# Four of the eight key tiles of each second query half leave TensorE's transposes: VectorE turns 32x32 squares, DRAM puts the squares in place

## The chip, the cores and the metric

The kernel runs on one core of a Trainium2 chip. The metric is the device time of one execution in microseconds (us), of which three were taken. One more execution was recorded by the hardware profiler; all rows below are from that one. Engines: PE is TensorE's matmul, PEld its weight load, DVE is VectorE, ACT is ScalarE, POOL is GpSimd, and SP is SyncE, which issues DMAs.

## The reference

Two layers are added to their input. x is (2, 1024, 512) in float32.

```python
xn = _layernorm(x)
# attention: 32 query heads of 128, 8 key/value heads, 4-bit weights with a scale for each group of 128 rows
q, k, v = [(qw - 8) * repeat(scales, 128)] products of xn, then rope on q and k
scores = q @ k.T / sqrt(128);  scores = where(causal, scores, finfo.min)
ctx = softmax(scores) @ v                       # float32
attn = ctx @ ((qw_o - 8) * repeat(scales_o, 128))
# linear layer: xn @ W_base.T + b_base, plus a top-2 mixture of 8 LoRA experts of rank 16
out = x + attn + ffn(xn)
```

The softmax over 1024 tokens is computed for 64 pairs of batch and query head (2 times 32), each with a causal mask.

## The kernel before

Every float32 product is made of three matmuls over a high and a low part (high times high, high times low, low times high). ACT makes the high part by a copy, DVE or POOL the low part by a subtraction.

Work is cut into 16 units (batch and key/value head), each with REP = 4 query heads. A head has two halves of 512 query tokens, c = 0 and c = 1. With causal masking, half 0 needs key tiles 0 to 3 and half 1 key tiles 0 to 7; tiles 0 to 3 of half 1 are full, tiles 4 to 7 hold the diagonal and get narrower (512, 384, 256 and 128 columns). For a head the steps on TensorE are:

- F: `project`, queries or keys of half c (12 matmuls of 512 columns), into one of the RING = 4 PSUM banks of `ring`. DVE makes three products for the rotary embedding (`terms`), POOL adds them (`rope_add`), ACT makes the high part (`rope_high`), POOL the low (`rope_low`).
- S: `scores` of query tile i against (i + 1) key tiles, 3 products. From i = 4 it takes two banks of `ring`. DVE copies it to `probs` with its mask and row maximum (`row_max`), ACT takes the exponential (`exps`).
- T: `turn`, up to four 128x128 transposes of probabilities for key tile j, into one of TURNS = 3 banks `turned`. ACT copies to `PT_high` (`high`), DVE subtracts for `PT_low` (`low`).
- V: `values`, the product of key tile j's probabilities and V, summed in the one bank `O_ps`. The first V of a half waits until DVE has taken the half before out of `O_ps` (`norm`, which multiplies by the reciprocal row sums in `R_sb`).
- O: `output`, context times output weights, added to Y by DVE (`add`). P: `rows_v`, rows of V for two units.

The order on TensorE is written by hand as strings of these letters: FIRST, EARLY and THIRD for half 0 of heads 0, 1 and 2, and 3; LATE and LAST for half 1. FIRST_P and LAST_P take the place of FIRST in even units and of LAST in odd ones. Every other engine runs one in-order queue. Its place for each operation comes from `behind(STEPS, us, kind)`, a rough clock of TensorE's steps: the operation is queued when the step is so many us old. A wait at the head of a queue holds all that stands behind it.

SP's queue holds all DMAs of the steady part: `load_weight` (two loads of 256 KB for each of 160 weights), `store_sums` and `load_sums` (the reciprocal sums go through DRAM to be spread over the partitions into `R_sb`). POOL scales each weight and splits it (four instructions, 3.8 us in sum).

## Time and profile before

| | us |
|---|---|
| device time, median of 3 | 2106.51 (2105.98 to 2108.94) |
| device time of the profiled execution | 2108.06 |
| its span, first to last instruction | 2106.3 |
| PE busy | 2084.7 (99%) |
| DVE / POOL / ACT busy | 1510.7 / 1213.4 / 993.5 |
| granted TensorE clock, mean | 0.998 |

The profiled execution's own time is 1.8 us over its span and 1.55 us over the median. Matmuls overlap in the trace (each has a duration that holds its way through the array), so what one costs is the distance from its start to the next start.

### The profile page before, as it was taken

The numbers are of one execution on the slowest core, as the hardware profiler recorded it, in microseconds if no ns is written. First come the engines' busy times: TensorE is split into PE (matmuls) and PEld (weight loads), VectorE is DVE, ScalarE is ACT, GpSimd is POOL, SyncE is SP. The second block draws the span as 40 slices with busy tenths as digits, with TensorE's granted clock in tenths as the row PEclk, the third lists the DMA queues.
The fourth block names the chain that finished last, engine by engine and source line by source line (L and its number), as shares of the span: only waits on it lengthen the run. The fifth ranks groups of instructions, "written<-read, shape, count | busy, mean of one in ns | idle before, by whom it ended". The sixth has DMA issues, their size and how long they took to land.

```text
span 2106.3 us, 31748 instructions
## 1 busy us (share of the span) xinstructions
PE 2084.7 (99%) x11690; PEld 1806.4 (86%) x11692; DVE 1510.7 (72%) x3056; ACT 993.5 (47%) x2199; POOL 1213.4 (58%) x1117
## 2 busy tenths in 40 slices
PE   8999999999999999999999999999999999999999
PEld 6888888888888888888888888888888888888887
DVE  6757776777767777677767777677776777767776
ACT  3145454554544545454444445454544545445453
POOL 3745665556655566456664666555665656646542
PEclk9999999999999999999999999999999999999999
DMA  6522222322312233232363422222231224313112
GB/s 222 156 41 61 58 69 56 61 56 56 81 46 57 59 61 76 44 67 58 61 149 80 114 59 63 49 71 61 56 78 34 71 46 79 73 31 70 36 41 66
DMA packets 160923, 145.88 MB, mean 69 GB/s; under 512 B 26368, under 2 KB 117248, under 8 KB 160256
## 3 DMA queue, kind: packets, MB, share of 16 engines
q1 hardware_dynamic: 157312, 137.80, 28.3%
q0 software_dynamic: 2112, 4.19, 0.6%
q8 instruction: 93, 1.52, 0.3%
q10 hardware_dynamic: 1344, 1.85, 0.3%
q14 instruction: 62, 0.51, 0.1%
HBM read 133.06 MB, written 10.75 MB: 68 GB/s over the span
## 4 chain that ended last, share of the span: by engine, by line
PE 94%; DVE 3%; POOL 1%; issue 1%; ACT 1%; DMA 0%; SPq 0%; DVEq 0%; POOLq 0%
PE ring L1123 43%; PE ring L1253 20%; PE O_ps L1123 19%; PE turned L1264 11%; POOL rope L683 1%; DVE rope L991 0%; POOL Q_low L691 0%; DVE rope L993 0%; DVE PT_low L924 0%; DVE stats L880 0%; DMA Y<-in_x 0%; DVE rope L992 0%; PE turned L1168 0%; ACT Q_high L736 0%; DVE xnT_low L924 0%
## 5 line engine op out<-in xcount | busy, mean ns | idle before, releaser
L736 ACT ACTIVATE PT_high<-turned 128x512 fp32r<-128x512 f32 (+3 forms) x771 | 359.2, 488 | 516.1 <-PE turned L1264 496.1
L790 ACT ACTIVATE probs<-probs,negmax 128x128 f32<-128x128 f32 (+7 forms) x512 | 398.1, 777 | 229.6 <-DVE negmax L1002 222.5
L924 DVE TENSOR_TENSOR PT_low<-turned,PT_high 128x512 fp32r<-128x512 f32 (+3 forms) x771 | 410.5, 555 | 117.0 <-ACT PT_high L736 108.6
L1002 DVE CUSTOM_DVE_ANT_0 probs<-ring,mask_row 128x128 f32<-128x128 f32 (+7 forms) x512 | 386.0, 754 | 83.1 <-PE ring L1253 74.2
L698 POOL TENSOR_TENSOR ctx_low<-ctx_f,ctx_high 128x512 fp32r<-128x512 f32 x128 | 165.4, 1292 | 410.0 <-ACT ctx_high L736 410.0
L1264 PE MATMUL turned<-ident,probs 128*128 128x128 f32 x2304 | 344.5, 273 | 0.0
L683 POOL TENSOR_TENSOR rope<-rope 128x512 f32<-128x512 f32 x160 | 206.9, 1293 | 177.0 <-DVE rope L993 175.9
L1264 PEld LDWEIGHTS turned<-ident,probs 128*128 128x128 f32 x2304 | 273.2, 140 | 35.5
L1123 PE MATMUL O_ps<-PT_high,V_high 128*128 128x512 f32 (+3 forms) x768 | 284.9, 371 | 7.1 <-DVE PT_low L924 7.1
L1043 DVE TENSOR_TENSOR Y<-ring,Y 128x512 f32<-128x512 f32 x256 | 177.0, 692 | 126.0 <-PE ring L1123 121.8
L1123 PE MATMUL O_ps<-PT_high,V_low 128*128 128x512 f32 (+3 forms) x768 | 265.9, 346 | 0.0
L1123 PE MATMUL O_ps<-PT_low,V_high 128*128 128x512 f32 (+3 forms) x768 | 265.1, 345 | 0.0
L1123 PE MATMUL ring<-xnT_high,W_high 128*128 128x512 f32 x640 | 255.2, 399 | 0.0
L1123 PE MATMUL ring<-xnT_high,W_low 128*128 128x512 f32 x640 | 250.0, 391 | 0.0
L1123 PE MATMUL ring<-xnT_low,W_high 128*128 128x512 f32 x640 | 249.5, 390 | 0.0
L1253 PE MATMUL ring<-K_high,Q_high 128*128 128x384 f32 (+5 forms) x768 | 236.7, 362 | 3.7 <-POOL Q_low L691 3.7
L1253 PE MATMUL ring<-K_low,Q_high 128*128 128x384 f32 (+5 forms) x768 | 221.4, 342 | 0.0
L1253 PE MATMUL ring<-K_high,Q_low 128*128 128x384 f32 (+5 forms) x768 | 221.3, 342 | 0.0
L691 POOL TENSOR_TENSOR Q_low<-rope,Q_high 128x512 fp32r<-128x512 f32 x128 | 165.5, 1293 | 94.3 <-ACT Q_high L736 93.1
L991 DVE TENSOR_TENSOR rope<-ring,cos_sb 128x512 f32<-128x512 f32 x160 | 110.7, 692 | 147.4 <-PE ring L1123 145.4
L649 POOL TENSOR_TENSOR W_low<-scl,W_high 128x512 fp32r<-128x512 f32 x160 | 206.8, 1292 | 13.3
L634 POOL TENSOR_TENSOR scl<-raw,scl 128x512 f32<-128x512 f32 x160 | 206.7, 1292 | 13.3
(115 smaller groups left out, 3861.1 us busy)
## 6 DMA issues: line engine op xcount, KB each, us to landing
R_sb<-row_sums SPq DMA_DIRECT2D x128, 256.0 KB, 4.1
raw<-in_qw_q SPq DMA_DIRECT2D x64, 256.0 KB, 4.8
scl<-in_scales_q SPq DMA_DIRECT2D x64, 256.0 KB, 8.6
raw<-in_qw_o SPq DMA_DIRECT2D x64, 256.0 KB, 4.5
scl<-in_scales_o SPq DMA_DIRECT2D x64, 256.0 KB, 4.8
raw<-in_qw_k SPq DMA_DIRECT2D x16, 256.0 KB, 4.5
scl<-in_scales_k SPq DMA_DIRECT2D x16, 256.0 KB, 6.1
raw<-in_qw_v SPq DMA_DIRECT2D x16, 256.0 KB, 4.4
```

The source lines that it names most:

```text
L634: own(nc.gpsimd.tensor_tensor(out=scl[:, n % 2, :], in0=as_float, in1=scl[:, n % 2, :], op=ALU.mult))
L649: nc.gpsimd.tensor_tensor(out=W_low[:, slot, :], in0=scl[:, n % 2, :], in1=W_high[:, slot, :].bitcast(f32), op=ALU.subtract).then_inc(w_do ...
L683: nc.gpsimd.tensor_tensor(out=rope_a[:, n % 2, :], in0=rope_a[:, n % 2, :], in1=rope_b[:, n % 2, :], op=ALU.add).then_inc(rope_sum, 1)
L691: nc.gpsimd.tensor_tensor(out=low[:, half(c)], in0=rope_a[:, n % 2, :], in1=high[:, half(c)].bitcast(f32), op=ALU.subtract).then_inc(rope_ ...
L736: return nc.scalar.activation(dst, src, ACT.Copy)
L790: nc.scalar.activation(probs[:, at], probs[:, at], ACT.Exp, bias=negmax[:, i:i + 1], scale=-1.0, accum_out=sums[:, i:i + 1]).then_inc(exp_ ...
L924: nc.vector.tensor_tensor(out=dst, in0=src, in1=high.bitcast(f32), op=ALU.subtract).then_inc(pt_low, 1)
L1002: nc.vector.tensor_tensor_reduce(probs[:, prob_at[i]:prob_at[i] + n], score_place(u, h, i), mask_row[:, TOKENS - n:TOKENS], -1.0, -MASKED, ...
L1043: nc.vector.tensor_tensor(out=Y[:, t, :], in0=place(step), in1=Y[:, t, :], op=ALU.add).then_inc(ring_read, 1)
L1123: mm = nc.tensor.matmul(dst, lhs, rhs, start=start and n == 0, stop=stop and n == len(terms) - 1)
L1253: mm = nc.tensor.matmul(ps[:, lo:hi], lhs[:, tile], keys[:, lo:hi], start=first, stop=last)
L1264: mm = nc.tensor.transpose(turned_place(step)[:, q * P:(q + 1) * P], probs[:, at:at + P], ident[:, :])
```

## The change

For half 1 of every head, key tiles 0 to 3 no longer pass through `turn`. Instead:

1. `scores` of tiles i = 4 to 7 read the first 512 keys in another order (four groups of 32 keys from each of four tiles: `p (j b k) -> p b j k`). Its two matmuls for each product are now 512 columns and the rest; they were two halves of the width.
2. After the exponential, DVE transposes the first 512 columns of the row in place, in squares of 32 (`turn_squares`, four for a head).
3. SP writes these 256 KB to DRAM (`move_out`, four for a head) and reads them back in four DMAs of 256 KB (`move_in`) with partition and block exchanged, in runs of 128 floats. All four stores have to land first.
4. ACT makes `moved_high` (two buffers) and POOL, no longer DVE, `moved_low`; four each for a head.
5. `values` of half 1 run in the order 0, 1, 4, 5, 6, 7, 2, 3. LATE and LAST hold four T in place of eight, and all eight S of the next head stand in them; before, four of the eight stood in the next EARLY.
6. To make room: `PT_low` has 2 buffers (3 before), so `low` waits for the V of two turns ago; W has 9 slots (11); `raw` and `rope_b` have one buffer (two), so a weight's load waits until POOL has scaled the one before.
7. `store_sums` and `row_sums_inverted` follow the first T that is left in a half.

```diff
-EARLY = "S T T F V S T V S S T O O V V"
-THIRD = "T S F T V S T S S T V V O O V"
-LATE = "S T T T S F V T V T V O V T T V T S S O V T V V V"
+FIRST = "F T T V T O T V F O V O V O"
+EARLY = "F T F T T O V O V O T O V V"
+THIRD = "F T F O T O V F T V T V O V F O"
+LATE = "S S T T V V S T V S T S V S V S V S V V"
+LAST = "T V S T T V S V S T V V S V S S S S V V"
+VALUES = ([0, 1, 2, 3], [0, 1, 4, 5, 6, 7, 2, 3])
+MOVED = 4
...
-            return (i + 1) * P // (2 if i >= 4 else 1)
+            return min(i + 1, MOVED) * P
...
+            def move_out(u, h, i):
+                n = head_of(u, h)
+                if seen.new(squared, 4 * n + i - 3):
+                    sp.wait_ge(squared, 4 * n + i - 3)
...
+                sp.dma_start(squares[n % 2][i - 4].rearrange("p (b n) -> p b n", b=4),
+                             row_squares(i).rearrange("p (b n) -> p b n", b=4)).then_inc(moved_out[i - 4], 16)
...
+            def move_in(u, h):
+                n = head_of(u, h)
+                for i in range(4):
+                    if seen.new(moved_out[i], 16 * (n + 1)):
+                        sp.wait_ge(moved_out[i], 16 * (n + 1))
...
+                back = squares[n % 2].rearrange("r (a k) (b n) -> b k (r a) n", a=4, b=4)
+                for b in range(4):
+                    sp.dma_start(moved[32 * b:32 * (b + 1), :, :, :].rearrange("p t j q -> p t (j q)"),
+                                 back[b]).then_inc(moved_in[n % 2], 16)
...
+            squares_out, squares_in = behind(STEPS, 4.5, "scores"), behind(STEPS, 6.5, "scores")
...
+                nc.gpsimd.tensor_tensor(out=low, in0=moved[:, :, j, :], in1=high.bitcast(f32),
+                                        op=ALU.subtract).then_inc(moved_done, 1)
...
+            def turn_squares(u, h, i):
+                need = score_number[u, h, i]
+                if seen.new(exp_done, need):
+                    dve.wait_ge(exp_done, need)
+                nc.vector.transpose(row_squares(i), row_squares(i)).then_inc(squared, 1)
...
-                at = slice(max(0, j - 4 * c) * P, HALF)
-                mm = product(O_ps[:, at], [(both(V_high, V_low, slice(None), u % 2, j),
-                                            both(PT_high, PT_low, slice(None), j % TURNS, at))],
-                             start=j == 0, stop=last)
...
+                if j < 4 * c:
+                    turned_tile = moved_high[:, j % 2, :], moved_low[:, j % 2, :]
```

**First place, DVE where an even unit ends and an odd one begins.** Before: the last row maximum of LAST (512 columns, tile 3), the context of the half (`ctx_f`), an `add`, a projection's three products, then the low part of FIRST's first turn.

```order
L1002 ISA probs,negmax<-ring,mask_row 128x512 [waits ring_full]
L1002 ISA negmax 128x1
L1032 TENSOR_TENSOR ctx_f<-O_ps,R_sb 128x512 [waits ctx_done,r_loaded,o_full]
L1043 TENSOR_TENSOR Y<-ring,Y 128x512 [waits ring_full]
L991 TENSOR_TENSOR rope<-ring,cos_sb 128x512 [waits rope_done,ring_full]
L992 TENSOR_TENSOR rope<-ring,sin_sb 64x512
L993 TENSOR_TENSOR rope<-ring,sin_sb 64x512
L924 TENSOR_TENSOR PT_low<-turned,PT_high 128x512 [waits pt_high]
```

Now, at the same place:

```order
L1156 STREAM_TRANSPOSE probs<-probs 128x512 [waits exp_done]
L1149 ISA probs,negmax<-ring,mask_row 128x1024 [waits moved_out3,ring_full]
L1149 ISA negmax 128x1
L1156 STREAM_TRANSPOSE probs<-probs 128x512 [waits exp_done] x3
L1184 TENSOR_TENSOR ctx_f<-O_ps,R_sb 128x512 [waits ctx_done,r_loaded,o_full]
L1129 TENSOR_TENSOR rope<-ring,cos_sb 128x512 [waits rope_done,ring_full]
L1133 TENSOR_TENSOR rope<-ring,sin_sb 64x512 [waits rope_sum]
L1134 TENSOR_TENSOR rope<-ring,sin_sb 64x512
L1062 TENSOR_TENSOR PT_low<-turned,PT_high 128x512 [waits valued,pt_high]
```

The widest row maximum and the square transposes, the last of which waits for the widest exponential, now stand ahead of that low part. On TensorE FIRST begins `F T T V` (it was `T F V`).

**Second place, SP in one head.** Now: four stores, the reciprocal sums of the next half 0, then the four loads, the next weight and the loaded sums.

```order
L569 DMA squares<-probs 128x512 [waits moved_in0,squared]
L569 DMA squares<-probs 128x512 [waits squared] x3
L544 DMA row_sums<-rinv 128x4 [waits r_loaded,rinv_ready]
L583 DMA moved<-squares 32x16x128 [waits moved_out3,moved_out2,moved_done,moved_out1,moved_out0]
L583 DMA moved<-squares 32x16x128 x3
L531 DMA raw<-in_qw_q 128x4x128 [waits scaled]
L535 DMA scl<-in_scales_q 128x4x128 [waits w_done]
L559 DMA R_sb<-row_sums 128x512 [waits ctx_made,r_stored]
```

Before, only the rows for sums and weights stood there. In most heads the sums' store stands ahead of the loads as here; in some it stands behind.

**Third place, TensorE where EARLY ends and LATE begins.** Now: S of tiles 0 and 1, two turns (seven transposes), then the first two V of the moved tiles.

```order
L1412 MATMUL ring<-K_high,Q_high 128x256 [waits ring_read]
L1412 MATMUL ring<-K_low,Q_high 128x256
L1412 MATMUL ring<-K_high,Q_low 128x256
L1423 MATMUL turned<-ident,probs 128x128 [waits exp_done]
L1423 MATMUL turned<-ident,probs 128x128 x6
L1278 MATMUL O_ps<-moved_high,V_high 128x512 [waits ctx_made,moved_done]
L1278 MATMUL O_ps<-moved_low,V_high 128x512
L1278 MATMUL O_ps<-moved_high,V_low 128x512
L1278 MATMUL O_ps<-moved_high,V_high 128x512 [waits moved_done]
```

Before, LATE had a projection (F, 12 matmuls) ahead of its first V. That V waits for two things: `ctx_made` (DVE has emptied `O_ps`) and `moved_done` (POOL's low part).

## Rows read from the trace of the kernel before

**Rows 1.** The page: busy time, and the chain that ended last by engine.

```profile
PE 2084.7 (99%) x11690; PEld 1806.4 (86%) x11692; DVE 1510.7 (72%) x3056; ACT 993.5 (47%) x2199; POOL 1213.4 (58%) x1117
...
PE 94%; DVE 3%; POOL 1%; issue 1%; ACT 1%; DMA 0%; SPq 0%; DVEq 0%; POOLq 0%
```

**Rows 2.** Busy time by stretch (us, busy and count by engine), two units' length.

```profile
489.00:738.00 249.00, 247.88 (x1394) 215.64 (x1393) 180.26 (x356) 120.86 (x268) 148.11 (x137) 1.00 0.26 60
```

**Rows 3.** Timeline of PE around two turns: start, us, engine, line, operation.

```profile
1035.58 0.39 PE L1123 MATMUL O_ps<-PT_high,V_low 128*128 128x512 f32 x1
1035.81 0.60 PE L1264 MATMUL turned<-ident,probs 128*128 128x128 f32 x4
1036.16 0.48 PE L1123 MATMUL O_ps<-PT_high,V_high 128*128 128x512 f32 x1
1036.48 0.40 PE L1123 MATMUL O_ps<-PT_low,V_high 128*128 128x512 f32 x1
```

**Rows 4.** Timeline of PE at scores of tiles 0 and 4.

```profile
1030.36 0.27 PE L1253 MATMUL ring<-K_high,Q_high 128*128 128x128 f32 x1
1030.47 0.27 PE L1253 MATMUL ring<-K_low,Q_high 128*128 128x128 f32 x1
...
1045.27 0.51 PE L1253 MATMUL ring<-K_high,Q_high 128*128 128x320 f32 x2
...
1045.91 0.46 PE L1253 MATMUL ring<-K_high,Q_low 128*128 128x320 f32 x2
```

**Rows 5.** Groups by line and shape, DVE: count, busy us, mean ns.

```profile
L924 DVE TENSOR_TENSOR PT_low<-turned,PT_high 128x512 fp32r<-128x512 f32 x387 | 260.9, 688 | 57.8 <-ACT PT_high L736 50.9
...
L1032 DVE TENSOR_TENSOR ctx_f<-O_ps,R_sb 128x512 f32<-128x512 f32 x128 | 138.6, 1083 | 25.0 <-PE O_ps L1123 23.8 <-issue 1.2
L992 DVE TENSOR_TENSOR rope<-ring,sin_sb 64x512 f32<-64x512 f32 x160 | 110.8, 693 | 2.1
...
L1002 DVE CUSTOM_DVE_ANT_0 probs<-ring,mask_row 128x1024 f32<-128x1024 f32 x64 | 78.4, 1225 | 18.1 <-PE ring L1253 17.4
...
L915 DVE MEMSET mask_row<- 128x448 uint32 x1 | 0.4, 432 | 0.0
```

**Rows 6.** The same view, ACT and POOL.

```profile
L736 ACT ACTIVATE Q_high<-rope 128x512 fp32r<-128x512 f32 x128 | 80.3, 627 | 117.9 <-POOL rope L683 116.9
L790 ACT ACTIVATE probs<-probs,negmax 128x1024 f32<-128x1024 f32 x64 | 73.6, 1150 | 23.7 <-DVE negmax L1002 23.7
...
L698 POOL TENSOR_TENSOR ctx_low<-ctx_f,ctx_high 128x512 fp32r<-128x512 f32 x128 | 165.4, 1292 | 410.0 <-ACT ctx_high L736 410.0
```

**Rows 7.** DMA view: SP's queue (packets, MB, share); issues (KB, us to landing).

```profile
q1 hardware_dynamic: 157312, 137.80, 28.3%
...
raw<-in_qw_q SPq DMA_DIRECT2D x64, 256.0 KB, 4.8
scl<-in_scales_q SPq DMA_DIRECT2D x64, 256.0 KB, 8.6
Y<-y_parked SPq DMA_DIRECT2D x2, 1024.0 KB, 5.0
out<-Y SPq DMA_DIRECT2D x8, 256.0 KB, 2.0
```

**Rows 8.** Timeline of SP: what issuing a DMA takes.

```profile
1035.36 0.43 SPq L495 DMA_DIRECT2D raw<-in_qw_v  x1
```

**Rows 9.** Timeline, a V that waits for a low part behind DVE's rope products.

```profile
478.66 0.60 PE L1264 MATMUL turned<-ident,probs 128*128 128x128 f32 x4
479.17 1.45 DVE L924 TENSOR_TENSOR PT_low<-turned,PT_high 128x512 fp32r<-128x512 f32 x2
479.92 0.50 PE L1123 MATMUL O_ps<-PT_high,V_high 128*128 128x512 f32 x1 [0.66 <-DVE PT_low L924]
```

**Rows 10.** Waits: who waited for whom, us in total, times, longest.

```profile
PE O_ps L1123 <- DVE PT_low L924: 7.1, 12, 1.0
PE ring L1253 <- POOL Q_low L691: 3.7, 8, 0.5
```

More of the change, by code:

```diff
@@ L117, in tensor_order @@
     steps += [("project", 0, w, c) for w in ("k", "q0") for c in range(2)]
-    steps += [("rows_v", 0, t) for t in range(NT)]
-    steps += [("scores", 0, 0, i) for i in range(4)]
+    steps += [("rows_v", 0, t) for t in VALUES[1]]
+    steps += [("scores", 0, 0, i) for i in range(NT)]
     for u in range(UNITS):
@@ L287, in build_program @@
         PT_high = sb("PT_high", [P, TURNS, HALF], f32r)
-        PT_low = sb("PT_low", [P, TURNS, HALF], f32r)
+        PT_low = sb("PT_low", [P, LOWS, HALF], f32r)
+        moved = sb("moved", [P, 16, MOVED, 32])
+        moved_high = sb("moved_high", [P, 2, HALF], f32r)
+        moved_low = sb("moved_low", [P, 2, HALF], f32r)
         ctx_high = sb("ctx_high", [P, CONTEXTS, HALF], f32r)
@@ L677, in add_bias, with moved_tile_low @@
                                         op=ALU.add).then_inc(bias_added, 1)
+            moved_order = itertools.count(1)
+            def moved_tile_low(u, h, j):
+                need = 4 * head_of(u, h) + j + 1
+                assert next(moved_order) == need
+                if seen.new(moved_high_done, need):
+                    pool.wait_ge(moved_high_done, need)
+                high, low = (ap[:, j % 2, :].rearrange("p (t q) -> p t q", t=16) for ap in (moved_high, moved_low))
+                nc.gpsimd.tensor_tensor(out=low, in0=moved[:, :, j, :], in1=high.bitcast(f32),
+                                        op=ALU.subtract).then_inc(moved_done, 1)
             def rope_add(u, w, c):
@@ L707, in _ @@
             added = behind(STEPS, 0.0, "lora_a")
+            moved_due = [behind(STEPS, us, "scores") for us in (11.0, 11.7)]
+            multiplied = behind(STEPS, 0.8, "values")
             for n in range(len(STEPS) + 1):
@@ L716, in _ @@
                         add_bias(b, t - 4)
-                for _, u, w, c in rotated_high[n]:
+                for _, u, w, c in (x for x in rotated_high[n] if x not in rotated[n]):
                     rope_low(u, w, c)
@@ L817, in _ @@
             projected, rotated = behind(STEPS, 0.1, "rows_v"), behind(STEPS, 4.0, "project")
+            moved_due = [behind(STEPS, us, "scores") for us in (10.0, 10.7)]
+            multiplied = behind(STEPS, 0.1, "values")
             divided, low_rank = behind(STEPS, 1.2, "values"), behind(STEPS, 0.1, "lora_a")
@@ L842, in _ @@
                     exps(u, h, i)
+                for j, due in enumerate(moved_due):
+                    for _, u, h, i in due[n]:
+                        if i == 7:
+                            moved_tile_high(u, h, j)
+                for _, u, h, c, j in multiplied[n]:
+                    if c and j < 2:
+                        moved_tile_high(u, h, j + 2)
                 for _, u, t in projected[n]:
@@ L1252, in scores @@
                     for lo, hi in banks:
-                        mm = nc.tensor.matmul(ps[:, lo:hi], lhs[:, tile], keys[:, lo:hi], start=first, stop=last)
+                        moving = keys[:, lo:hi]
+                        if i >= 4 and lo == 0:
+                            moving = moving.rearrange("p (j b k) -> p b j k", j=MOVED, b=4)
+                        mm = nc.tensor.matmul(ps[:, lo:hi], lhs[:, tile], moving, start=first, stop=last)
                 mm.then_inc(ring_full, 1)
```

232 lines of the change are left out of this document (162 added, 70 removed).

## The prediction

> **What bounds the kernel now.** I read busy time and the chain first. PE is busy 99% of the span and 94% of the chain [rows 1]; in a stretch of 249 us, two units or eight heads, it is busy 247.88 us at full clock (1.00, that is 2.4 GHz) [rows 2]. The list of waits confirms it: the largest of PE on DVE is 7.1 us in all, on POOL 3.7 us [rows 10]. So what is taken from PE comes off the span, unless a new wait takes its place. The other engines have room in the mean, 58% to 72%, but each is one in-order queue, so what counts is what stands ahead of an operation for which PE waits. The reader sees such a case in the timeline: a V starts 0.90 us late (0.66 of it shown as idle) because its low part stood behind rope products on DVE [rows 9]. That is where I look for the change's price.
>
> **What PE loses and gains.** A full turn starts at 1035.81 and the next matmul at 1036.16: 0.35 us. The matmul behind it then takes 0.32 to the next start where one of 512 columns otherwise takes 0.23 [rows 3]. So a turn costs 0.44 us, and 4 in each of 64 heads are gone: 256 x 0.44 = **-112.6 us**. Scores of tile 4 were six matmuls of 320 columns, 0.93 us with the one that follows a V (two starts of a pair's halves from 1045.27 to 1045.91, 0.64, and a third pair of 0.29) [rows 4]. They become three of 512 and three of 128: 3 x (0.23 + 0.11) = 1.02, so +0.1 x 64 = **+6 us** [rows 3, 4]. Tiles 5 to 7 keep their columns at 256 or more in each matmul; I take 0. The keys are now read in runs of 32, and no row shows a strided moving operand. Lower bound 0. The upper bound is the nearest strided read in a row, DVE's `norm`, 1.083 where a plain product takes 0.69, 57% more [rows 5]: on 4 x 3 x 0.23 = 2.8 us of scores a head that is 1.6 us, 100 us in all. I take 0, since that row is of another engine, and leave the upper end to rival D.
>
> **What the other engines get.** DVE loses 256 low parts of 0.688 and gains 256 square transposes of 128x512. No row shows one. Below stands the memset of 448 columns, 0.43; above the slowest product of 512, 1.08; I take 0.65, near the low parts and plain products of 0.69, since nothing here comes from PSUM [rows 5]. DVE's sum stays about where it was. The Trainium skill (VectorE: DVE Perf Modes, TRN2 errata) gives 58 cycles plus one an element for SBUF to SBUF, an estimate of 0.59 us; by it the sum below would be some 6 us lower. ACT keeps its count of copies. POOL gains 256 x 1.292 = 331 us [rows 6]: 1213 + 331 = 1544 of some 2040, 76%, not a bound. DMA gains 2 MB a head, 134 MB beside the 137.8 that took 28.3% [rows 7]; below 60% together.
>
> **Walk through one head change, zero at the end of S7** (the last scores of a head). DVE's row maximum of tile 7 takes 1.225 + 0.08 and ends at about 1.9 (it stands behind a square transpose); the exponential takes 1.15 + 0.19 and ends at 3.3; the last square transpose waits for it and ends at 4.0; `norm` 1.08, to 5.1; the rope products 3 x 0.69, to 7.2; the first low part, to 7.9 [rows 5, 6]. All that was not ahead of this low part before.
>
> *FIRST, 8 odd units.* PE does V V (1.4), F (12 x 0.23 = 2.7) and T T (0.7) and wants its V at 4.9. The low part is there at 7.9. PE waits 3.0 us: 8 x 3.0 = **+24 us**. In FIRST_P, EARLY and THIRD more work stands ahead of V (9 us and more): 0.
>
> *EARLY to LATE, heads 1 and 2, 32 times.* Two things are late by nearly the same. (a) `norm` of the half that just ended. Its V ends as LATE's S begins; on DVE the row maximum of S0 (0.37, started when S0's third matmul is out, 0.5 after its first start) stands ahead of it, then 1.08. It ends 2.0 us after LATE begins, and V is wanted at 1.4 (S S T T). Late by about 0.7. (b) The moved tiles. The reciprocal sums are ready at 8.1, behind the low part; SP's queue holds their store ahead of the loads [second place in the change], though the square stores have landed by 4.1 + 2.0 [rows 7]. Four loads are issued at 0.4 to 0.5 us each from 8.4 [rows 8]; a load of 256 KB in runs of 512 B lands 4.8 after its issue [rows 7], so the last at 14.7. ACT's copy 0.63, POOL's subtraction 1.29 [rows 6]: tile 0 is there at 16.8, tile 1 at 18.1. PE wants them at 16.7 and 17.4 (V V 1.4, two F 5.5, ten transposes 1.1, four O of six matmuls 5.5, four V 1.9, S S T T 1.4, with 0.23 for 512 columns and 0.11 for 128 [rows 3, 4]). With (a) the two overlap, and the longer counts: 0.8 us, 32 x 0.8 = **+26 us**. In FIRST and THIRD there is more work on PE or a wait already, so that I take 0 there.
>
> *LAST, 8 even units:* four S of two banks each stand in a row; the third needs the first's bank. DVE needs 0.9 to 1.3 us for each, PE 1.0 to 1.4. **+3 us.**
>
> *What goes away.* Where the wait of [rows 9] stood, eight times 0.9, and the scores of tile 4 that waited for POOL's `Q_low`, eight times about 0.5 [rows 9, 10], the order is another, with no rope products or projection close ahead: **-12 us**.
>
> Single buffers of `raw` and `rope_b`, and two of `PT_low`: a low part waits for a V that stands one or two steps behind its turn. In LATE that holds DVE 0.7 us, ahead of the row maximum of tile 4, and the bank is wanted 2 us later: 0. A weight's load now follows POOL's scaling; weights are due every 10 us and POOL's work on one is two such products of 1.29 and two shorter instructions [rows 6]: 0, as long as POOL is not late by more than about 2 us.
>
> **Sum:** 2106.3 - 112.6 + 6 + 24 + 26 + 3 - 12 = 2040.7 of span, 2042.5 of the profiled execution's own time. That execution lay 1.55 us over the median: **2041 us**, 3.1% less.
>
> **Rivals.**
>
> *A, the forecast*, 0.48. Its own range is 2020 to 2065: transposes of 0.5 to 0.8, a last load that lands 0.5 us sooner or later.
>
> *B, the waits are absorbed*, 0.17. DVE and the loads keep ahead, PE waits only where it did. 2106.5 - 112.6 + 6 = 2000, or 1992 to 2015. For it speaks that PE's waits before were under 1%; against it the walk, in which three waits follow from orders and durations.
>
> *C, the same waits, longer*, 0.24. If a square transpose takes 1.08 (upper bound) the chain has three of them behind the last row maximum or beside it: +1.3 us at 40 places, +52: 2093. If the four loads queue behind each other (1 MB lands 5.0 after one issue [rows 7], and here other loads may still run), the last is 1 us later, +32: 2073. Range 2065 to 2100.
>
> *D, slower than before*, 0.10. One mechanism: `move_in`'s landing. Each microsecond that it is late is a microsecond of PE in 32 heads, since ACT's copy, and all that stands behind it on ACT, waits for it at the head of the queue. It decides from (2106.5 - 2041) / 32 = 2.0 us: if the last load lands 6.8 and not 4.8 after its issue. The scales' loads, also in runs of 512 B, take 8.6 [rows 7]; with that, 2041 + 32 x 3.8 = 2163. Against it: those loads stand behind the raw weights' each time and read one row for all partitions. Keys read at the strided rate (above) would end here too: 2041 + 100.
>
> *E, a rule against the change*, 0.01, inside D. The store and the load with exchanged partitions are a plain DMA with strides. If each 512 B run cost 19 times its time, the 4.8 us would be 91 us, three heads' time, and the kernel 64 x 91 = 5800 us. The raw query weights are also read in runs of 128 columns, and their 256 KB land in 4.8, no later than 1 MB of whole rows (5.0); so the row speaks for 4.8 [rows 7]. The rule is in the Trainium skill (VectorE: DVE Perf Modes, The three transpose paths: a plain DMA that transposes by access-pattern strides is 19 times slower "when the innermost dest stride is large"). The innermost stride here is one element.
>
> **How the numbers follow.** A measurement of this kernel tells about 0.2% (4 us) from no change. B and A lie below 2102 in full, C too; of D nearly all lies above 2111. Faster 0.88, within 0.2% 0.03, slower 0.09. The range that leaves out no more than 2 in 10 reaches from B's lower part to C's upper part: 2000 to 2092.
>
> **What the profile after would show.** T groups: 1280 transposes at L1423 and not 2304. STREAM_TRANSPOSE x256 with its mean, 0.65 or not. Waits of PE or PEld at `O_ps`: on DVE `PT_low`, about 3 us eight times (FIRST); on DVE `ctx_f` or POOL `moved_low`, under 1 us in 32 heads. If the second list is longer than 26 us, the landing of `moved<-squares` (I say 4.8) tells C from D. SP's wait for `rinv` ahead of the loads shows whether (b) is right. Wrong I would be if POOL, at 76%, ran late as a whole: its waits for `moved_high` would then be short and PE's for W or Q long; or if scores of tiles 4 to 7 showed starts further apart than 0.23.

## The result, and the profile after

| | before | after |
|---|---|---|
| device time, median of 3 (us) | 2106.51 | 2406.54 (2401.65 to 2408.05) |
| span of the profiled execution | 2106.3 | 2399.8 |
| mean granted TensorE clock | 0.998 | 0.939 |

The ratio is 1.1416, 95% interval 1.1394 to 1.1439: 14% slower, where 3% faster was forecast. The page, against [rows 1]:

```profile
span 2399.8 us, 31278 instructions
PE 2110.1 (88%) x10668; PEld 1781.4 (74%) x10668; DVE 1500.1 (63%) x3056; ACT 977.1 (41%) x2199; POOL 1521.5 (63%) x1373
...
q1 hardware_dynamic: 329344, 272.05, 44.1%
...
PE 32%; DMA 26%; DVE 14%; issue 11%; ACT 6%; POOL 6%; SPq 4%; DVEq 0%
```

PE was 94% of the chain and is 32%; DMA was 0% and is 26%. PE now waits. The list of waits (engine and line, who released it, us in all, times, longest), against [rows 10]:

```profile
ACT moved_high L835 <- DMA moved<-squares: 439.9, 64, 15.2
DVE PT_low L1062 <- ACT PT_high L835: 292.5, 133, 12.1
PE O_ps L1278 <- DVE PT_low L1062: 221.1, 74, 11.3
...
PE O_ps L1278 <- DVE ctx_f L1184: 37.4, 26, 3.8
...
PE O_ps L1278 <- POOL moved_low L763: 7.9, 2, 7.1
...
SPq L531 <- POOL scl L705: 501.0, 81, 14.4
```

Read the first three as a chain. PE hardly ever waits for a moved tile (7.9 us). It waits for `PT_low`, the low part of an ordinary turned tile; DVE makes that late because ACT's copy `PT_high` is late; and ACT is late because it stands in front of a moved copy whose loads have not landed, in every one of 64 heads. PE's matmul groups by shape say which tile suffers: in half 0, V of tile 2 has 256 columns and V of tile 3 has 128.

```profile
L1278 PE MATMUL O_ps<-PT_high,V_high 128*128 128x256 f32 x128 | 41.2, 322 | 90.7 <-DVE PT_low L1062 79.8 <-DVE V_low L1161 10.8
...
L1278 PE MATMUL O_ps<-PT_high,V_high 128*128 128x128 f32 x128 | 36.2, 283 | 114.9 <-DVE PT_low L1062 114.7
```

One place shows all of it. The timelines of SP, ACT and PE (start, us, engine, operation):

```profile
1516.73 3.57 SPq L569 DMA_DIRECT2D squares<-probs  x3
1523.73 0.32 SPq L544 DMA_DIRECT2D row_sums<-rinv  x1
1527.52 2.00 SPq L583 DMA_DIRECT2D moved<-squares  x4
1529.62 0.43 SPq L559 DMA_DIRECT2D R_sb<-row_sums  x1
...
1525.70 0.49 ACT L835 ACTIVATE PT_high<-turned 128x384 fp32r<-128x384 f32 x1 [0.76 <-PE turned L1423]
1534.40 1.15 ACT L835 ACTIVATE moved_high<-moved 128x512 fp32r<-128x512 f32 x2 [8.21 <-DMA moved<-squares]
1535.46 0.61 ACT L835 ACTIVATE Q_high<-rope 128x512 fp32r<-128x512 f32 x1
1535.98 0.53 ACT L835 ACTIVATE PT_high<-turned 128x256 fp32r<-128x256 f32 x2
...
1531.05 0.27 PE L1423 MATMUL turned<-ident,probs 128*128 128x128 f32 x1
1536.85 0.58 PE L1278 MATMUL O_ps<-PT_high,V_high 128*128 128x256 f32 x1 [5.53 <-DVE PT_low L1062]
```

PE turned tiles 2 and 3 by 1531.3. ACT could have copied them at once, but stood at the head of its queue from 1526.2 until the loads landed at 1534.4, and PE stood from 1531.3 to 1536.85. Two more things are in these rows. The last store of squares was issued at 1519.98, yet SP could issue the first load only at 1527.5, after that store had landed. And the load of `R_sb`, the row sums of the half that is being computed, is issued behind the four moved loads.

The same stretch in windows (busy time of PE, PEld, DVE, ACT, POOL; then the granted clock, DMA share and GB/s):

```profile
1525.00:1531.30 6.30, 6.30 (x32) 5.02 (x30) 3.63 (x7) 0.49 (x1) 3.79 (x3) 1.00 0.47 112
1531.30:1536.80 5.50, 0.02 (x1) 0.00 (x0) 1.71 (x4) 2.10 (x5) 1.69 (x2) 0.91 0.89 225
1536.80:1542.50 5.70, 5.65 (x16) 4.75 (x17) 1.90 (x3) 0.45 (x1) 5.53 (x6) 0.50 0.01 1
1542.50:1550.00 7.50, 7.50 (x46) 6.62 (x45) 3.65 (x8) 2.48 (x7) 7.33 (x8) 0.99 0.02 2
```

After the wait of 5.5 us PE runs 5.7 us at 0.50, the lower of its two levels, 1.2 GHz. Matmuls of 512 columns start 0.43 us apart there, not 0.23. The wait of 5.5 us costs some 2.8 us more, half of those 5.7. (The Trainium skill, TensorE: Matmul & The Clock Gate, Part 1, names these two levels, beside a third that needs three busy cores of a die, and counts the loss as half of the time at the lower one; the window agrees.)

**Where 293.5 us of span went.** I took the starts of all matmuls in both traces and gave each the distance that its form has when nothing waits. That work is 2058 us before and 1950 after: -108. What stands beyond it ahead of the first matmul of each V is 11 us before, 310 after: +299. What stands beyond it anywhere else is 32 before and 134 after: +102, nearly all of it between matmuls at the lower clock, at which the trace has 291 us in all (7 before). Sum +293.

### The profile page after: what moved, and what is told of

Its sections match the earlier page's. It is cut to its first block, busy times and chain, and to the rows that moved or that the text cites. A ratio compares the mean times of both kernels' runs of the same rounds, so it can differ in the third digit from the quotient of the medians.

```text
span 2399.8 us, 31278 instructions
## 1 busy us (share of the span) xinstructions
PE 2110.1 (88%) x10668; PEld 1781.4 (74%) x10668; DVE 1500.1 (63%) x3056; ACT 977.1 (41%) x2199; POOL 1521.5 (63%) x1373
## 4 chain that ended last, share of the span: by engine, by line
PE 32%; DMA 26%; DVE 14%; issue 11%; ACT 6%; POOL 6%; SPq 4%; DVEq 0%
DMA moved<-squares 11%; PE O_ps L1278 10%; PE ring L1412 10%; PE ring L1278 10%; DMA R_sb<-row_sums 8%; DMA squares<-probs 5%; DVE probs L1149 4%; DVE ctx_f L1184 3%; SPq L583 3%; ACT probs L909 3%; PE turned L1423 2%; DVE probs L1156 2%; ACT moved_high L835 2%; DVE PT_low L1062 2%; DMA row_sums<-rinv 1%
## 5 line engine op out<-in xcount | busy, mean ns | idle before, releaser
L1062 DVE TENSOR_TENSOR PT_low<-turned,PT_high 128x512 fp32r<-128x512 f32 (+3 forms) x515 | 250.1, 491 | 381.1 <-ACT PT_high L835 292.5
L763 POOL TENSOR_TENSOR moved_low<-moved,moved_high 128x512 fp32r<-128x512 f32 x256 | 324.0, 1280 | 244.6 <-ACT moved_high L835 243.5
L835 ACT ACTIVATE PT_high<-turned 128x512 fp32r<-128x512 f32 (+3 forms) x515 | 216.9, 430 | 296.8 <-PE turned L1423 276.4
L835 ACT ACTIVATE moved_high<-moved 128x512 fp32r<-128x512 f32 x256 | 151.3, 624 | 451.8 <-DMA moved<-squares 439.9
L1412 PE MATMUL ring<-K_high,Q_high 128*128 128x512 f32 (+3 forms) x768 | 242.0, 369 | 0.2
L1412 PE MATMUL ring<-K_high,Q_low 128*128 128x512 f32 (+3 forms) x768 | 230.5, 354 | 0.0
L1412 PE MATMUL ring<-K_low,Q_high 128*128 128x512 f32 (+3 forms) x768 | 230.5, 354 | 0.0
L1423 PE MATMUL turned<-ident,probs 128*128 128x128 f32 x1280 | 224.9, 292 | 0.0
L1278 PE MATMUL ring<-W_high,ctx_high 128*128 128x512 f32 x512 | 218.8, 427 | 0.5 <-POOL W_low L725 0.5
L725 POOL TENSOR_TENSOR W_low<-scl,W_high 128x512 fp32r<-128x512 f32 x160 | 206.4, 1290 | 13.3
L705 POOL TENSOR_TENSOR scl<-raw,scl 128x512 f32<-128x512 f32 x160 | 206.2, 1289 | 13.3
L1278 PE MATMUL ring<-W_high,ctx_low 128*128 128x512 f32 x512 | 209.2, 409 | 0.0
```

The costliest lines, as they stand in the source:

```text
L705: nc.gpsimd.tensor_tensor(out=scl[:, n % 2, :], in0=as_float, in1=scl[:, n % 2, :], op=ALU.mult).then_inc(scaled, 1)
L725: nc.gpsimd.tensor_tensor(out=W_low[:, slot, :], in0=scl[:, n % 2, :], in1=W_high[:, slot, :].bitcast(f32), op=ALU.subtract).then_inc(w_do ...
L763: nc.gpsimd.tensor_tensor(out=low, in0=moved[:, :, j, :], in1=high.bitcast(f32), op=ALU.subtract).then_inc(moved_done, 1)
L835: return nc.scalar.activation(dst, src, ACT.Copy)
L1062: nc.vector.tensor_tensor(out=dst, in0=src, in1=high.bitcast(f32), op=ALU.subtract).then_inc(pt_low, 1)
L1278: mm = nc.tensor.matmul(dst, lhs, rhs, start=start and n == 0, stop=stop and n == len(terms) - 1)
```

## The experiments

All medians are of the timed runs, each beside the kernel before (2106.1 to 2108.9 in these sessions). In the tables "V3 h1" is the mean wait of PE, per head, ahead of V of tile 3 of half 0 of head 1 of a unit, "V0' h1" that ahead of V of moved tile 0 in half 1, from the same starts.

### First round: the place of the wait, the trip, the weight loads

`act_16` moves two places in two queues (capped so that they stay ahead of V of tile 0); `act_13` has 13.0, 13.7, 14.0, 14.7:

```diff
-            moved_due = [behind(STEPS, us, "scores") for us in (10.0, 10.7)]     # ACT
+            moved_due = [moved_due_at(STEPS, us) for us in (16.0, 16.7)]
...
-            moved_due = [behind(STEPS, us, "scores") for us in (11.0, 11.7)]     # POOL
+            moved_due = [moved_due_at(STEPS, us) for us in (17.0, 17.7)]
```

> Only the places of the first two moved tiles in two queues change: ScalarE's copies go from 10.0 and 10.7 us to 16.0 and 16.7 us behind the scores of tile 7, GpSimd's low parts from 11.0 and 11.7 to 17.0 and 17.7, so that ScalarE's copies of the first half's four turned tiles stand ahead of the wait for the loads (they stood behind it for one or two tiles of each head). TensorE's order, the transfers and all buffers stay. Theory 1 (the head of ScalarE's queue waits for the loads and holds turned tiles behind it): ScalarE's wait for the moved loads falls from 440 us to under 150, TensorE's waits for PT_low from 479 us to under 200, and the time falls by 150 to 300 us, to 2110 to 2260. Theory 2 (the trip through DRAM is too long for the tiles themselves): the waits move to the moved tiles (moved_low, now 8 us), and the time stays above 2350. Theory 3 (what costs is something else, such as the single raw buffer, two low slots or the order): within 30 us of 2407.

> The same edit, half as far: ScalarE's copies of moved tiles 0 and 1 at 13.0 and 13.7 us, GpSimd's low parts at 14.0 and 14.7. In the planner's time the first half's turns end at 7.6 to 17.5 us behind the scores of tile 7, the fourth of most heads at 13.9, so the fourth tile's copy still stands behind the wait in most heads. Theory 1 (it matters what stands behind the waiting copy, not how long ScalarE has other work): little is won, 20 to 100 us, time 2310 to 2390, and ScalarE still waits over 250 us for the loads. If instead the time falls in proportion to the move (half of what the move to 16.0 gives), what matters is the amount of work that is left ahead of the wait.

`trip_once`: `move_out` and `move_in` return at once for all heads but the first.

> The squares are stored and loaded for the first head alone; for the other 63 the four stores and four loads are left out, and the moved copies read what the first head left (so the key tiles 0 to 3 of the second halves are multiplied by the first head's probabilities). Squares of 32, copies, products, order and buffers stay. Theory 1 and 2 (waiting for the trip is what costs, at the head of ScalarE's queue or anywhere): the waits of ScalarE for the loads (440 us) and of TensorE for PT_low and moved_low go to under 60 us together, and the time is 2020 to 2090. Theory 3 (something else of the change costs as much): it stays above 2200, and the difference to 2060 is what the rest of the change costs.

`weights_5`: `weights_due(STEPS, -8.0)` of SP becomes `-5.0`.

> The weight loads stand at 5 us ahead of their due time in SyncE's queue, not at 8; in the profile SyncE waits 501 us for GpSimd's scaling of the weight before (one raw buffer) at these loads. Nothing else moves. If SyncE's queue makes the moved loads late (rival: sums, weights and their waits stand ahead of them), the loads are issued sooner for the fourth head of each unit (now 10.8 to 12.9 us behind the row maximum, against 7.5 in the others) and the time falls by 20 to 80 us. By theory 1, whose loads wait for the stores' landing at 7.1 us in any case, it moves by less than 20 us: three heads of four have the same issue times.

| | us | V3 h1 | V3 h2 | V2 h3 | V0' h0 | V0' h1 | V0' h2 |
|---|---|---|---|---|---|---|---|
| the change | 2406.5 | 3.4 | 3.7 | 5.2 | 1.3 | 1.3 | 0.3 |
| act_13 | 2413.0 | 3.1 | 3.1 | 5.7 | 2.3 | 1.8 | 0.4 |
| act_16 | 2447.1 | 0.4 | 0.2 | 2.0 | 3.4 | 6.6 | 3.0 |
| trip_once | 2194.9 | 0.3 | 0.3 | 2.0 | 0.7 | 2.6 | 0.8 |
| weights_5 | 2500.7 | 3.8 | 4.9 | 7.6 | 0.0 | 0.1 | 0.0 |

Theory 1 was right about the place and wrong about the price. With T3's copy ahead of the wait V3 hardly waits (0.4 and 0.2 us), but the time rises: the wait reappears at V of moved tile 0, and the time stays above 2350, as theory 2 had said. In `act_16`:

```profile
PE O_ps L1289 <- POOL moved_low L774: 187.9, 43, 14.4
PE O_ps L1289 <- DVE PT_low L1073: 87.1, 56, 4.9
...
L715 POOL TENSOR_SCALAR raw<-raw 128x512 f32<-128x512 int32 x160 | 99.1, 619 | 201.1 <-DMA scl<-in_scales_q 124.7 <-DMA scl<-in_scales_o 29.0 <-DMA scl<-in_scales_v 26.9
```

Part of it is the new place on POOL, behind the scaling of a weight that has not landed. `act_13` fits theory 1 in its tiles (T3's copy still stands behind, V3 still waits) and wins nothing. `trip_once` bounds the trip: 2406.5 - 2194.9 = 212 us are the trip through DRAM; 88 us over the kernel before are the rest of the change, though it has 108 us less work. That lies between what theories 1 and 2 (to 2090) and theory 3 (from 2200) had said. `weights_5` contradicts both sides of what I expected: moving SP's weight loads 3 us costs 94 us. GpSimd waits 190 us for weights (62 in the change), and the moved loads are issued later, not sooner, in heads 0, 2 and 3 (10.2, 9.6 and 12.7 us behind the row maximum against 7.7, 8.2 and 9.4). There the last store of squares takes 5.9, 5.9 and 9.0 us to land (3.3, 3.7 and 5.0 in the change). So the tiles that stand behind ACT's wait suffer more.

### Second round: traffic or waiting, and POOL's place

`traffic_only` keeps all stores and makes the loads from DRAM to DRAM; ACT does not wait for them; SP waits for those of the head before ahead of the next:

```diff
-                    sp.dma_start(moved[32 * b:32 * (b + 1), :, :, :].rearrange("p t j q -> p t (j q)"),
+                    sp.dma_start(moved[...] if n == 0 else aside_dram[b],
```

> Behind the first head, the four loads of each head write the same bytes in the same runs of 512 B to a place in DRAM instead of the tile moved, and ScalarE no longer waits for them (the key tiles 0 to 3 of second halves are multiplied by the first head's probabilities). Stores, order, places and buffers stay. Against the kernel without the transfers (2195 us): if the transfers cost only because somebody waits for their landing, the time is the same, 2180 to 2215. If they cost as traffic too (weights, sums and their waits come later, since SyncE's queue and the DMA engines are shared), it lies above, 2230 to 2330, with GpSimd's wait for weight loads and SyncE's waits grown. Over 2350 would mean that ScalarE's wait hardly matters.

`pool_ahead`: as `act_16`, with POOL's places 15.5 and 16.2.

> As the kernel with the copies at 16.0 and 16.7 us, which took 2447 us, but GpSimd's low parts of moved tiles 0 and 1 at 15.5 and 16.2 us and not at 17.0 and 17.7, ahead of the scaling of weights that GpSimd waits for there (in the second head 3.5 us between ScalarE's copy and the low part). If what the later place won on ScalarE was lost to that wait on GpSimd, the low parts end 3 to 5 us sooner in the second head, the waits of TensorE for moved tiles fall from 6.3 and 6.9 us to 2 to 4 there, and the time is 2290 to 2400, below the changed kernel. If the wait comes from the landing itself, 2410 to 2460.

`halves`: `move_in` in two parts, behind the scores of tiles 5 and 7; `halves_16` has the places of `pool_ahead` too.

> The loads of a head are made in two parts: rows of tiles 4 and 5 as soon as these are stored (6.5 us behind the scores of tile 5), rows of tiles 6 and 7 as before; eight loads of 128 KB and not four of 256 KB, the same bytes. Half of the bytes are then in before the last store lands. If the bytes behind the last store set the landing, ScalarE's copy of moved tile 0 starts 2.5 to 4 us sooner (means 15.3 to 17.4 us behind the row maximum now), TensorE's waits at the first half's tile 3 in heads 1 and 2 (3.0 to 4.0 us each) fall to 0.5 to 1.5, and the time is 2270 to 2350. If the number of issues and stores' landing set it, the copy starts less than 1 us sooner and the time stays within 30 us of 2407.

> Both edits together: loads in two parts, ScalarE's copies of moved tiles at 16.0 and 16.7 us, GpSimd's low parts at 15.5 and 16.2. If the landing and what stands behind the waiting copy are together what the trip costs (212 us, by the kernel without transfers), the wait of ScalarE for the loads is under 60 us and the time is 2200 to 2280. If the traffic itself costs, 2300 to 2400.

Measured: `traffic_only` 2307.9, `pool_ahead` 2397.5, `halves` 2380.4, `halves_16` 2382.3 us. So the transfers cost 2307.9 - 2194.9 = 113 us with no engine but SP waiting for the moved loads, their places and waits in SP's queue included, and ACT's waiting for them 99 more. The waits show how that can cost. PE's list, first `trip_once`, then `traffic_only`:

```profile
PE O_ps L1282 <- DVE ctx_f L1188: 56.8, 39, 4.6
```

```profile
PE O_ps L1283 <- DVE ctx_f L1189: 148.7, 48, 12.7
```

`ctx_f` is the norm of half 0, which frees `O_ps` for V0'. It needs `R_sb`, and that load is issued behind the moved loads. This is a second wait: in the changed kernel it lies mostly behind the first, and in `act_16` and `pool_ahead` it comes out. `pool_ahead` gains 50 us on `act_16`, yet V0' h1 still waits 5.6 us. In `halves` the copies start 0.8 to 2.1 us sooner, less than expected, and 26 us are won: V3 waits 1.3 and 2.3 us in heads 1 and 2, but V0' h1 now 3.5. `halves_16` adds nothing. ACT waits only 67 us for the loads there, and PE 90 us for `ctx_f` and 84 us for `moved_low`.

### Third round: the row sums

`sums_early`: for half 0 alone, DVE's reciprocal and SP's store move ahead, and SP's load stands before the moved loads:

```diff
+                for _, u, h, i in sums_early[n]:        # behind(STEPS, 2.5, "scores")
+                    if i == 5:
+                        store_sums(u, h, 0)
...
+                for _, u, h, i in sums_due[n]:          # behind(STEPS, 5.0, "scores"), ahead of move_in
+                    if i == 7:
+                        load_sums(u, h, 0)
```

> The first half's row sums take another place: VectorE's reciprocal 1.0 us and SyncE's store 2.5 us behind the scores of tile 5, the load of R_sb 5.0 us behind those of tile 7, ahead of the moved loads, and not 1.0 and 4.0 us behind the half's first turn, where the load of R_sb stands behind the four moved loads and their wait. ScalarE's and GpSimd's places stay. Theory A (two waits one behind the other: ScalarE's wait for the loads, and behind it the norm of the first half, whose row sums come behind 1 MB of moved loads on the same queue): the norm's part is in the changed kernel mostly covered by ScalarE's wait, so the time falls by 20 to 70 us, to 2335 to 2385, with TensorE's waits for ctx_f under 15 us (37 now). Theory B (the sums don't matter): within 15 us of 2407.

`sums_16` adds the places of `pool_ahead`, `sums_halves_16` the loads in two parts as well.

> The same places of the row sums, and with them ScalarE's copies of moved tiles at 16.0 and 16.7 us and GpSimd's low parts at 15.5 and 16.2, which by themselves took 2397 us. Theory A: with both waits gone only the landing itself is left; TensorE's waits at the first moved tile of heads 1 and 2 fall from 5.9, 5.4, 1.0 and 3.5 us to under 2.5 us each, and the time is 2250 to 2330. Theory B: 2380 to 2410.

> The same once more, and the moved loads in two parts. Theory A, with the landing 1 to 3 us sooner: 2210 to 2300, and at least 15 us below the kernel with whole loads. If the traffic as such is the floor (2308 us in the kernel whose loads nobody waits for), not below 2290.

`weights_11`: `weights_due(STEPS, -11.0)`.

> The weight loads at 11 us ahead of their due time in SyncE's queue and not at 8, nothing else: the opposite of the kernel with 5 us, which took 2501 us. If that one lost because GpSimd waited for weights that came late (190 us for raw, 62 in the changed kernel), the time here is lower than 2407, 2340 to 2395, and GpSimd waits under 40 us. If it lost because other loads then stood in front of the moved ones in the fourth head, the place matters by chance and the time may rise: 2410 to 2450.

| | us | V3 h1 | V3 h2 | V2 h3 | V0' h0 | V0' h1 | V0' h2 |
|---|---|---|---|---|---|---|---|
| sums_early | 2349.8 | 1.7 | 4.3 | 4.2 | 0.0 | 0.4 | 0.2 |
| sums_16 | 2323.8 | 0.3 | 0.2 | 2.4 | 1.0 | 3.3 | 1.5 |
| sums_halves_16 | 2389.4 | 0.3 | 0.3 | 2.1 | 2.0 | 4.5 | 2.1 |
| weights_11 | 2612.0 | 11.4 | 3.4 | 5.6 | 5.0 | 0.0 | 0.1 |

Both times lie in theory A's ranges, though V0' h1 still waits 3.3 us where under 2.5 was expected. The row sums alone give 57 us and the later copies 26 on top, where by themselves they gave 9 (`pool_ahead`). Together that is 83 us against 66 if the two simply added; the difference of 17 us is hardly clear of its own 95% interval (some 16), so that the two waits overlap rests mainly on the tables, where V0' comes out as V3 goes. In `sums_early` V0' falls to 0.4 us and less, and V3 h2 rises to 4.3. DVE's group for the norm, in the change and in `sums_early` (idle before it after the last bar):

```profile
L1184 DVE TENSOR_TENSOR ctx_f<-O_ps,R_sb 128x512 f32<-128x512 f32 x128 | 135.3, 1057 | 72.5 <-DMA R_sb<-row_sums 42.3 <-issue 27.4 <-PE O_ps L1278 2.6
```

```profile
L1191 DVE TENSOR_TENSOR ctx_f<-O_ps,R_sb 128x512 f32<-128x512 f32 x128 | 135.3, 1057 | 9.1 <-DMA R_sb<-row_sums 7.0 <-PE O_ps L1289 2.1
```

`sums_halves_16` was a miss: 66 us worse than with whole loads. SP now waits for squares to land in the middle of its stores (348 us in all, against 185 in `sums_16`), and what stands behind is late; I did not separate this further. `weights_11` is the largest effect of any run, +205 us, for three microseconds in one queue. SP's waits there:

```profile
SPq L531 <- POOL scl L705: 664.0, 115, 14.4
SPq L544 <- DVE rinv L1172: 505.4, 67, 19.1
...
SPq L576 <- DMA squares<-probs: 195.3, 40, 10.0
```

In heads 0 and 1 the first moved load is issued 13.3 and 14.7 us behind the row maximum of tile 7, against 7.7 and 7.9 in the change. The last store of squares is itself issued late there (6.4 us behind the row maximum, 3.4 and 3.6 in the change) and then takes 6.7 and 6.2 us to land (3.3 and 2.8).

### Fourth round: the single raw buffer

`scales_first` splits a weight's two loads: scales at -13, integers at -6.

> A weight's two loads take places of their own in SyncE's queue: the scales (two buffers, up to 9.2 us from issue to landing) 13 us ahead of the due time, the integers (one buffer, wait for GpSimd's scaling of the weight before) 6 us ahead; both stood at 8 us. Everything else stays. Theory C (the single raw buffer costs as a wait at the head of SyncE's queue, with squares and moved loads behind it): SyncE's wait for the scaling falls from 501 us to under 200, GpSimd's wait for weights stays under 80 us, the copies of moved tiles start 1 to 3 us sooner in heads 1 to 3, and the time is 2320 to 2385. Without it (rival: these waits fall into time in which SyncE has nothing to issue), within 20 us of 2407.

The other three add it to `sums_early`, to `sums_16`, and to `sums_early` with the trip made once.

> The early row sums (2350 us by themselves) and the weights' loads at two places together, ScalarE's and GpSimd's places as in the changed kernel. If the two waits add up, 2270 to 2330; if they overlap, 2330 to 2350.

> The same with ScalarE's copies at 16.0 and 16.7 us and GpSimd's low parts at 15.5 and 16.2 (2324 us without the weights' two places). Theory C: TensorE's wait at the first moved tile of the second head in even units (6.0 us, GpSimd behind a weight) falls under 3 us, and the time is 2230 to 2300. Rival: 2310 to 2335.

> Squares stored and loaded for the first head alone, as in the kernel of 2195 us (key tiles 0 to 3 of the other second halves are multiplied by the first head's probabilities), with the early row sums and the weights' two places. The waits for ctx_f (57 us at the first moved tile) should be gone and those for V2 of the last head (2.0 us, 16 times) and V0 of the first head (2.6 us, 8 times) stay: 2120 to 2170. Under 2106 would mean that the change can win if its trip were free; over 2180 that the rest of it costs through the order itself.

Measured: `scales_first` 2473.2, `sums_scales` 2409.5, `sums_scales_16` 2364.9, `once_sums_scales` 2131.3 us. Theory C falls as it stood. The wait it blamed halved (501 to 228 us) and the time rose 67 us. But the edit gave SP a wait in its place, 127 us for POOL's split of a weight ahead of the scales' loads (14 in the change), so it shows what this split costs and not what a second raw buffer would win; no run has one. ACT's moved copy started at 19.0 and 19.2 us in heads 0 and 1 (15.3 and 16.7 in the change) and at 15.7 and 16.7 in heads 2 and 3 (16.5, 17.4): the heads that have weights' loads among their squares pay. In heads 0 and 1 the last store is issued no later than before (3.4 us) but takes 5.8 and 8.3 us to land (3.3 and 2.8). Added to the early sums the split costs as much (+60, +41). `once_sums_scales` is the lowest time that these edits reach (what the split costs without the trip, no run separates): 1.0101 of the kernel before (1.0074 to 1.0128). PE's waits in it:

```profile
PE O_ps L1298 <- DVE PT_low L1078: 64.0, 54, 2.4
PE O_ps L1298 <- DVE ctx_f L1200: 10.3, 31, 0.6
```

So even with the trip free of cost the waits of the new order, 99 us ahead of V from the starts, and the lower clock behind them (0.977) eat the 108 us of work saved. Two groups make most of the 64 us: FIRST, 2.6 us in 8 odd units, and THIRD, 2.0 us in 15 of 16 units ahead of V2, where the low part stands behind DVE's rope products:

```profile
861.53 0.69 DVE L1145 TENSOR_TENSOR rope<-ring,cos_sb 128x512 f32<-128x512 f32 x1 [2.61 <-PE ring L1298]
...
863.66 0.62 DVE L1078 TENSOR_TENSOR PT_low<-turned,PT_high 128x256 fp32r<-128x256 f32 x2
...
864.13 0.38 PE L1298 MATMUL O_ps<-PT_high,V_high 128*128 128x256 f32 x1 [1.78 <-DVE PT_low L1078]
```

One more part of the change stands in every run: with two buffers of `PT_low` DVE waits for a V of two turns ago, 84 us in the change and 107 here (no such row before). No run gives the third buffer back, so what that costs PE is open.

### Fifth round: weights on another queue

`sums_16_act` and `sums_16_pool` start from `sums_16` (2323.8). ACT, or POOL right behind its scaling, issues the weights' loads.

> Against the kernel with early row sums and later copies on ScalarE (2324 us): behind the third, the weights' loads are issued by ScalarE on its own queue, 7 us ahead of their due time and not 8, with their wait for GpSimd's scaling; SyncE's queue holds squares, sums and moved loads alone. Theory Q (squares and moved loads stand behind weights on one queue, in SyncE's order and in the queue's): the mean start of ScalarE's moved copy and its wait for the loads (about 60 to 110 us in all now) fall, SyncE waits no more for the scaling, and the time is 2230 to 2300. Rival (the wait for the scaling now holds ScalarE's exponentials and copies): slower, 2340 to 2450. Rival (bytes): 2310 to 2335.

> The same, but GpSimd issues the loads of the next weight itself right behind its scaling of the one before, so that no engine waits for the scaling; its four issues in the trace of the changed kernel took 0.74 to 0.95 us each, so 320 of them are 240 to 300 us more work on GpSimd, 63 to 76 per cent of its span. Theory Q: 2230 to 2310. If GpSimd's issues make the low parts of moved tiles and contexts late, 2330 to 2450, with TensorE's waits for moved_low over 200 us.

Measured: 2459.6 and 2446.4 us. SP no longer waits for the scaling in either. The issues and landings of `sums_16_act` (KB each, median us to landing):

```profile
squares<-probs SPq DMA_DIRECT2D x256, 256.0 KB, 4.6
moved<-squares SPq DMA_DIRECT2D x256, 256.0 KB, 5.4
...
scl<-in_scales_q ACTq DMA_DIRECT2D x63, 256.0 KB, 9.2
```

In `sums_16` these are 4.5, 4.8 and 9.0. With the weights off SP's queue squares and moved loads land no sooner, so theory Q falls for the landing. (The Trainium skill, DMA: Bandwidth & Descriptors, Issuing engines are not separate DMA queues, says that DMAs of all issuing engines run on the same 16 DMA engines, and that another issuing engine saves only issue time. The moved loads of both runs agree.) The price was on the issuers. ACT, with the waits for the scaling in its queue, let DVE wait 305 us for `PT_high` (116 in `sums_16`). POOL's busy time went from 1520 to 1747 us; ACT waited 446 us for its rope sums (332) and PE 174 us for `PT_low` (78); for `moved_low` it waited 105 us (119), not the over 200 expected. In `sums_16_pool` squares land sooner (2.8), but a moved load still takes 5.0. There part of theory Q holds: the first moved load is issued 5.7 to 7.2 us behind the row maximum (7.5 to 9.2 in `sums_16`), and ACT waits 28 us for the loads (81). The waits above put the loss on POOL's late work.

## Why the prediction was wrong

**What held.** PE's work: -112.6 + 6 = -106.6 forecast, -108 measured. T groups: 1280 as said. FIRST: 3.0 us eight times forecast, 2.6 measured in the change and 2.6 to 2.7 in the experiments. Keys read in runs of 32: scores start 0.23 to 0.24 apart (0.28 at the first of tiles 6 and 7), no strided cost; tile 4's six matmuls take 1.07, 1.02 forecast. LAST's 3 us for a bank did not show: the scores have 0.2 us of waits before them in all. `norm` late by 0.7 (a): 0.6 ahead of V0' in heads 1 and 2 once the sums are early and the trip is gone (`once_sums_scales`). Rival E did not come: 256 KB with partition and block exchanged land in a median of 5.0 us, not in 91. The square transpose: 0.65 taken,

```profile
L1156 DVE STREAM_TRANSPOSE probs<-probs 128x512 f32<-128x512 f32 x256 | 180.4, 707 | 41.1 <-ACT probs L909 37.0
```

0.707 measured. The table row of the Trainium skill (VectorE: DVE Perf Modes, The TRN2 errata) gave an estimate of 0.59, further off; the same section says that this row under-predicts and that some 150 cycles are fixed, an estimate of 0.69 here. A moved load: 4.8 said, 5.0 measured in the median of all 256, and by this number the forecast should have come. But the median mixes four places: the first to the fourth load of a head land 3.5, 4.3, 5.3 and 6.5 us after their issue. Rival D's condition spoke of the last load, 6.8 us, and in heads 1 and 2 the last takes 7.2 and 6.8. So D's condition was met there, and by D's price the time would have been 2041 + 32 x 2.2 = 2111, not 2407: D too had the price of the wait wrong.

**The step that failed first** is the end of the walk, EARLY to LATE (b): "tile 0 is there at 16.8 ... PE wants them at 16.7". It asked when the moved tile is wanted and not what stands behind ACT's copy of it while that copy waits. In the order of `behind`, the copy is queued at 10.0 us, and T3 of heads 1 and 2, T2 and T3 of head 3 come behind it. I had named this in rival D ("all that stands behind it on ACT, waits for it at the head of the queue") and priced it only from 2.0 us of lateness on. What it costs begins as soon as T3's tile waits, however late or early the moved tile itself is wanted. V3 waits 3.4 and 3.7 us in heads 1 and 2, V2 5.2 in head 3, of which 2.0 stay without the trip: 16 x (3.4 + 3.7 + 3.2) = 165 us, not 26. "In FIRST and THIRD ... I take 0 there" was wrong with it, by 2.0 us in 15 of 16 units even without the trip: the kind of wait that [rows 9] show, a low part behind rope products, stands in THIRD too.

**The landing.** Forecast 14.7 us behind S7's end for the last load. S7's end and the start of its row maximum lie 0.2 us apart here. ACT's copies start at 15.3, 16.7, 16.5 and 17.4 us behind the row maximum in heads 0 to 3. The term that was too small is the last load: 4.8 said, 6.1 to 7.2 measured from its issue to ACT's start, each later load of the four taking longer than the one before. Rival C had a microsecond for that. The stores' landing was wrong too: taken as 2.0, from stores of Y [rows 7], it is 3.8 in the median among weight loads and 7.4 in the example. It moved less than it seems, since the walk had the loads wait for the sums' store instead: the first was to be issued at 8.4, and is at 7.7, 7.9, 8.2 and 9.4 behind the row maximum. That these agree is luck.

**A term that was missing.** "(a) `norm` ... late by about 0.7" followed DVE alone. The load of `R_sb` stands behind the four moved loads on SP; `sums_early` shows it worth 57 us.

**Another missing term** is the clock. All waits were priced at their length. At a mean of 0.939, 2 x (1 - 0.939) x 2400 = 293 us lie at the lower level, which costs up to half of that, 146 us; the starts give +102 outside the waits themselves. It adds up to half of a wait's length to it (2.8 us on 5.5 in the example, 102 on 299 in sum), and short waits pay it as well: `once_sums_scales`, whose waits of PE for `PT_low` are none over 2.4 us, has a mean of 0.977, by the same sum 98 us at the lower level.

**The step on weights**, "A weight's load now follows POOL's scaling ... 0, as long as POOL is not late by more than about 2 us", asked whether the weight is in time. It is. What matters is when its 0.5 MB and its waits cross the squares and moved loads (`weights_5`, `weights_11`, `scales_first`). How much of the 113 us of traffic goes through the row sums and how much through slower landings, the runs do not fully separate; once the sums are early and the copies late (`sums_16`), 217 us over the kernel before remain, of them 193 over the kernel without the trip (`once_sums_scales`, which differs in the scales' place too).

## What to carry to other kernels

A transfer that must land in the middle of a tight order is to be priced three times: its own landing among the traffic of that stretch, everything behind the instruction that waits for it on that instruction's engine, and everything behind its issue on the issuing queue. Removing one of two waits that overlap may show little (9 us) or make it worse (41 us); try both together before calling either harmless. A shift of 3 us of unrelated loads moved this kernel by 94 and 205 us, so with DMA on the chain the places of all loads are one plan.

## What the runs showed of the hardware

- After a wait of PE of 5.5 us, PE ran 5.7 us at 0.50 of the clock; over the kernels the mean went down as the waits grew: 0.977 (`once_sums_scales`), 0.973 (`trip_once`), 0.939 (the change), 0.904 (`weights_11`).
- Of four loads of 256 KB in runs of 512 B, issued 0.4 to 0.6 us apart, the first lands 3.5 us after its issue and the fourth 6.5 (medians of the change); all are in 8.0 us after the first issue. With the weights' loads on another engine's queue the median of all four gets no shorter (5.4 and 5.0, 4.8 in `sums_16`). At half the size, 128 KB, it is 2.7 (`halves`). 256 KB in 5.0 us is 52 GB/s for one of several in flight; all DMA together moved 225 GB/s in the window above.
- A matmul whose moving operand is read in four groups of 32 columns from each of four tiles takes no longer to the next start than a plain one (0.23 to 0.24 us for 512 columns in tile 5; 0.28 at the first of tiles 6 and 7).
